# Moving Wout's second-half products of unit 0 three states apart from its gate, and two sums that take in more tiles, in a state-space block with a feed-forward block

## The chip, the cores and the metric

The program runs on one core of one Trainium2 chip. The metric is the device time of one execution in microseconds (us); for the kernel before it is the median of 3 runs, 1132.78 us (1132.46 to 1133.34). A core has five engines that run side by side, each through its own queue in the order of the program: TensorE (PE, matrix products), VectorE (DVE), ScalarE (ACT), GpSimd (POOL) and SyncE (SP, which only issues transfers here). They wait for each other through semaphores.

## The reference

The layer normalises `x` (4 batches of 512 rows of 512), and adds to `x` the output of a Mamba block and of a gated feed-forward block in fp8. Cut to what matters:

```python
def step(h, inp):                      # per time step, per channel (1024), per state (16)
    dA_t, dBu_t, C_t = inp
    h = dA_t * h + dBu_t
    y = jnp.einsum('bdn,bn->bd', h, C_t)
    return (h, y)
...
y = y + hs * D[None, :, None]
y = y * _silu(gate)
out = jnp.einsum('bdl,hd->blh', y, Wout)
...
activations = gelu(x8 @ w_gating[0]) * (x8 @ w_gating[1])   # fp8 operands
ffn = activations @ w_linear                                 # fp8 operands
return x + out + ffn
```

## The kernel before, in words

The program has two parts. `block_a` (to about 235 us) prepares everything; `block_b` runs the scan and all that depends on it, and the change is in `block_b` alone.

The 1024 channels are 8 tiles of 128. A **unit** is one tile `k` (0 to 7) of one batch `b` (0 to 3): 32 units in a row. In each unit there are 16 **states** `n`. For each state ACT makes `da` in a PSUM bank (an exponential, line 896), POOL makes `dbu` (a product, line 938) and DVE runs the scan over 512 time steps (line 995). Eleven states are multiplied by C on DVE (`prod`, line 964). Five, those of `POOLED` = 1, 4, 7, 9, 12, are scanned into `hp` and multiplied on POOL (line 949), `POOL_LAG` = 3 states later. PE sums all 16 products into the bank `yT` by transposing them against an identity (`add_state`, line 1115). When a unit is summed, ACT copies the sum to `y_t` (line 863), PE transposes it back (`back`, line 1033, at state 4 of the next unit), and DVE multiplies it by the gate into `y2` (`gated`, line 970, at state 7 of the next unit). `y2` holds 8 tiles, one for each unit of the batch.

Beside the scan PE makes other products into two PSUM banks `mm`. Which group is made at which state is written in tables, and `pe_pieces` (line 591) turns them into lists: an entry `first` puts a group's four parts at the states `first - 1` to `first + 2` of the unit, and entries at 0 or below come ahead of state 0. The groups:

- `ffn`: the fp8 products of the feed-forward (line 1073), six in unit 0. ACT copies each out of its bank (line 904), the first at its state 10, the sixth at state 15.
- `gate`: four f32 products (line 1085), read by ACT's Silu at state 6 of the next unit.
- `out_a`: Wout times tiles 0 to 3 of `y2`, for the four tiles `h` of the output, in units 5 and 6 of the same batch; DVE adds each to `acc` (line 976, at the states in `OUT_A_ADDED`).
- `out_b`: Wout times tiles 4 to 7, with the feed-forward's output added through an identity (`add_ffn`, line 1044), in units 0 to 3 of the next batch; DVE adds each to `acc` (line 982, at the states in `OUT_B_ADDED`) and SP stores it. It can't begin before unit 7's tile is in `y2`, which comes at state 7 of unit 0.
- `lin`: the feed-forward's second fp8 product (line 1094).

`bank_plan` (line 612) hands the two banks to the groups in turn, in the order of their first parts, and `take_bank` makes PE wait at a group's first part until the bank's last group has been read. All of it is one queue on PE: a part that waits holds up what is behind it, the summing of states too. DVE likewise takes a sum's addition in its place among the scans, and waits there if the sum isn't done. In batch 0 there is no `out_b` in units 0 to 3, since no batch went before.

In the last batch nothing follows unit 7. Its second half is begun inside unit 7 by `LAST` and `begin_last` (line 1124), in four banks named by `last_banks`, and the end of the program makes the rest: `back` for unit 7, tile 7's products, `add_ffn`, four additions and four stores.

Of the kernel before, what the change touches and what calls it, by code (L numbers as in the profile page):

```python
# [21 lines left out]
B, L, H = 4, 512, 512  # L22
# [3 lines left out]
HT = H // P  # L26
LT = L // P
KU = DI // P
# [16 lines left out]
SLOTS = 4  # L45
# [16 lines left out]
HIDS = (3, 3, 3, 3, 4)  # L62
FFN_UNITS, MOST = len(HIDS), max(HIDS)
FFN, FFN_COPIED = (5, 5, 5, 5, 4), (10, 10, 10, 10, 8)
OUT_B, OUT_B_ADDED = (11, -3, -3, -3), {(1, 0): 0, (1, 5): 1, (2, 5): 2, (3, 5): 3}
GATE = (12, 11, 11, 11, 12, 12, 12, 3)
OUT_A_LIN = {4: (), 5: (("out_a", 0, -3), ("out_a", 1, 4), ("lin", 0, 6), ("lin", 1, 9)),
             6: (("out_a", 2, -3), ("out_a", 3, 4), ("lin", 2, 7)), 7: (("lin", 3, 6),)}
MADE = {group[:2]: k for k in OUT_A_LIN for group in OUT_A_LIN[k]}
OUT_A_ADDED = {(5, 5): 0, (5, 9): 1, (6, 5): 2, (6, 9): 3}  # L70
LIN_COPIED = {(5, 14): 0, (6, 1): 1, (6, 15): 2, (7, 14): 3}
GELU_USED, PORT_GIVEN = 4, 4
BACK = 4

LAST = {8: ((1, 4),), 9: ((1, 5), (1, 6)), 11: ((0, 4), (0, 5)), 12: ((0, 6),), 13: ((3, 4), (3, 5)), 14: ((3, 6), (2, 4)),
        15: ((2, 5),)}


def build(nc, x, xT, win_hs, win_gate, wdt, wx, cols, alog, wffn, wout, outT):
# [546 lines left out]
def block_b(nc, xT, win_gate, wout, outT, ident, neg_a, skip, ahead, dram):  # L626
# [9 lines left out]
    plan = bank_plan()  # L636
    with ExitStack() as ctx:
# [34 lines left out]
        da = [ps(f"da{i}", [P, L]) for i in range(SLOTS)]  # L672
        yT = [ps(f"yT{i}", [P, L]) for i in range(2)]
        mm = [ps(f"mm{i}", [P, L]) for i in range(BANKS)]
        last_banks = [mm[plan[(KU - 1, "lin", HT - 1)][0]], yT[0], mm[plan[(KU - 1, "gate", 0)][0]], da[12 % SLOTS]]

        wout_loaded, wlin_loaded = sem("wout_loaded"), sem("wlin_loaded")
        b_loaded = [sem(f"b_loaded{g}") for g in range(G)]
# [9 lines left out]
        y_t_ready, back_mm, y2_ready = sem("y_t_ready"), sem("back_mm"), sem("y2_ready")  # L688
# [339 lines left out]
        def _(pe):  # L1028
# [4 lines left out]
                    ins = nc.tensor.transpose(yT[k % 2][:, t * P:(t + 1) * P], y_t[:, t * P:(t + 1) * P], ident[:, :])  # L1033
                ins.then_inc(back_mm, 1)

            def project_out(bank, h, c, first):
                return nc.tensor.matmul(bank[:, :], wout_sb[:, c, h * P:(h + 1) * P], y2[:, c, :],  # L1037
                                        start=(c == first), stop=(c == KU // 2 - 1))

            def add_ffn(bank, b, h):  # L1040

# [17 lines left out]
            def beside(b, k, piece, opening):  # L1059

                name, h, c = piece
                if name == "out_b" and opening:
                    return
                if name == "ffn":
# [5 lines left out]
                    bank = take_bank(b, k, (name, h), opening)  # L1070
                    pe.sem_inc(waited, 1)
                    for f in range(HT):
                        ins = nc.tensor.matmul(bank[:, :], wffn[:, k % 2, j, f, s, :].bitcast(FP8), xn8[:, f, :].bitcast(FP8),  # L1073
                                               start=(f == 0), stop=(f == HT - 1))
# [4 lines left out]
                bank = group_bank[name]  # L1079
                if name == "gate":  # L1080
                    if c == 0:
                        pe.wait_ge(wgate_loaded[k % 2], unit_loads(b, k))
                        if k == 0:
                            pe.wait_ge(xnT_loaded, b * 16 + 16)
                    ins = nc.tensor.matmul(bank[:, :], wgate[:, k % 2, c * P:(c + 1) * P], xnT[:, c, :],  # L1085
                                           start=(c == 0), stop=(c == 3))
                    done = gate_mm
                elif name == "lin":
                    if c == 0:
                        pe.wait_ge(wlin_loaded, b * 16 + 16)  # L1090
                        pe.wait_ge(act8_ready, b * FFN_UNITS + FFN_UNITS)
                        pe.sem_inc(waited, 1)
                    for i in range(4 * c, 4 * c + 4):
                        ins = nc.tensor.matmul(bank[:, :], wlin[:, i, h * P:(h + 1) * P].bitcast(FP8), act8[:, i, :].bitcast(FP8),  # L1094
                                               start=(i == 0), stop=(i == HID // P - 1))
                    done = lin_mm
                elif name == "out_a":
                    if c == 0:
                        pe.wait_ge(wout_loaded, 16)
                        pe.wait_ge(y2_ready, b * KU + KU // 2)  # L1100
                    ins = project_out(bank, h, c, 0)
                    done = out_a_mm
                else:
                    if c == 0:
                        pe.wait_ge(y2_ready, b * KU)
                    ins = project_out(bank, h, KU // 2 + c, KU // 2)
                    if c == 3:
                        ins = add_ffn(bank, b - 1, h)
                    done = out_b_mm
# [7 lines left out]
                return ins  # L1117

            def begin(h, c):
                project_out(last_banks[h], h, c, KU // 2)  # L1120

            def begin_last(n):

                if n == 8:
                    pe.wait_ge(y2_ready, B * KU - 1)
                if n == 11:
                    pe.wait_ge(lin_copied, B * HT)
                if n == 13:
                    pe.wait_ge(scanned, (B * KU - 1) * N + 12 + 1)
                if n == 14:  # L1130
                    pe.wait_ge(sg_ready, B * KU)
                for h, c in LAST[n]:
                    begin(h, c)
# [36 lines left out]


            back(B * KU - 1, KU - 1)
            begin(2, 6)
            pe.wait_ge(y2_ready, B * KU)
            for h in range(HT):
                project_out(last_banks[h], h, KU - 1, KU // 2)
# [36 lines left out]
```

## Time and profile before

| what | value |
| --- | --- |
| median of 3 runs | 1132.78 us |
| the profiled execution: its time | 1132.28 us |
| the profiled execution: its span | 1130.5 us |
| busy over the span | DVE 92%, POOL 82%, PE 81%, ACT 69% |
| busy in 459 to 682 us, 223 us of the scan | DVE 217.46, POOL 208.74, PE 185.01, ACT 158.24 us |
| TensorE's granted clock, mean | 0.929 of 2.4 GHz |

The span runs from the first to the last instruction; the execution's own time is 1.8 us longer. A timeline row has the start in us, the duration in us, the engine, the line, the instruction, output and input, and a count where equal instructions were merged. Brackets give the idle time of the engine just before it and what ended that. Two instructions of one engine overlap by some 0.1 us where the next begins as the last drains, so a row of two scans of 1.21 us each reads 2.33 us. An f32 product of 128x512 is two MATMUL records (x2), a fp8 one is four for a whole sum (x4), a state's sum is four transposes (x4).

### The profile page before, as it was taken

How to read it: one execution, taken by the hardware profiler on the slowest of the kernel's cores; microseconds unless marked ns; L12 is line 12 of the kernel's file. 1: busy time of each engine (PE TensorE's matmuls, PEld its weight loads, DVE VectorE, ACT ScalarE, POOL GpSimd, SP SyncE). 2: the span in 40 equal slices, each digit the busy share in tenths (PEclk: the TensorE clock that was granted, in tenths of full speed). 3: DMA queues.
4: the chain of work that ended last, by engine and by line, in shares of the span. 5: the costliest groups of instructions: out<-in, count | busy, mean ns of one | idle time of the engine just before them, and what ended most of it. 6: DMA issues, size and time to landing. Idle time of an engine off the chain costs nothing.

```text
span 1130.5 us, 14619 instructions
## 1 busy us (share of the span) xinstructions
PE 921.0 (81%) x4272; PEld 568.1 (50%) x4272; DVE 1041.6 (92%) x1242; ACT 782.7 (69%) x1118; POOL 928.4 (82%) x752
## 2 busy tenths in 40 slices
PE   4878789757777897888888978887988798878988
PEld 3646466334444454555444554444554454454544
DVE  6968777679999999999999999999999999999995
ACT  4687877657778666777785557777856677778552
POOL 5343425489999999989998999999999989999993
PEclk9999999968889999799989989999899899989999
DMA  7677777981111217432212183421212922212101
GB/s 273 207 255 230 285 221 290 374 334 53 52 57 38 84 38 261 177 117 70 75 38 68 55 299 120 130 75 57 71 51 70 347 90 72 75 57 75 38 1 38
DMA packets 53158, 150.24 MB, mean 133 GB/s; under 512 B 5728, under 2 KB 14048, under 8 KB 50016
## 3 DMA queue, kind: packets, MB, share of 16 engines
q1 hardware_dynamic: 53088, 149.41, 38.4%
q8 instruction: 32, 0.52, 0.2%
q14 instruction: 38, 0.31, 0.1%
HBM read 111.37 MB, written 38.01 MB: 132 GB/s over the span
## 4 chain that ended last, share of the span: by engine, by line
POOL 51%; DVE 14%; issue 7%; PE 5%; ACT 1%; DVEq 0%; POOLq 0%
POOL dbu L938 38%; POOL hp L949 14%; DVE hp L995 4%; DVE da L995 3%; DVE prod L964 3%; DVE gate_bf L1011 2%; DVE act L1014 2%; PE mm L1037 2%; PE yT L1115 1%; PE mm L1085 1%; ACT da L896 0%; PE mm L1094 0%; PE da L1037 0%; PE yT L1037 0%; ACT unit L858 0%
## 5 line engine op out<-in xcount | busy, mean ns | idle before, releaser
L896 ACT ACTIVATE da<-unit,neg_a 128x512 f32<-128x512 f32 x512 | 339.0, 683 | 216.5 <-DVE prod L964 215.9
L938 POOL TENSOR_TENSOR dbu<-unit,b_head 128x512 f32<-128x512 f32 x384 | 478.1, 1279 | 3.5 <-POOLq L103 3.5
L995 DVE TENSOR_TENSOR_SCAN da<-da,dbu 128x512 f32<-128x512 f32 x352 | 418.5, 1215 | 8.3 <-POOL dbu L938 6.7
L1115 PE MATMUL yT<-ident,prod 128*128 128x128 f32 x1408 | 237.3, 298 | 138.5 <-DVE prod L964 137.9
L1115 PEld LDWEIGHTS yT<-ident,prod 128*128 128x128 f32 x1408 | 174.9, 151 | 272.8 <-DVE prod L964 220.6
L949 POOL TENSOR_TENSOR hp<-hp,c_head 128x512 f32<-128x512 f32 x128 | 163.4, 1277 | 52.3 <-DVE act L1014 46.3
L995 DVE TENSOR_TENSOR_SCAN hp<-da,dbu 128x512 f32<-128x512 f32 x160 | 193.0, 1206 | 7.9 <-ACT da L896 7.9
L964 DVE TENSOR_TENSOR prod<-da,c_head 128x512 f32<-128x512 f32 x256 | 170.5, 666 | 0.0
L938 POOL TENSOR_TENSOR dbu<-unit,b_all 128x512 f32<-128x512 f32 x128 | 160.3, 1278 | 0.0
L1073 PE MATMUL mm<-xn_b,w_sb 128*128 128x512 fp8e4 x512 | 150.1, 429 | 3.1 <-ACT gate_bf L904 2.0
L1085 PE MATMUL mm<-xnT_b,wgate 128*128 128x512 f32 x256 | 130.1, 606 | 8.1 <-ACT gate_bf L904 8.0
L1037 PE MATMUL mm<-y,wout_sb 128*128 128x512 f32 x240 | 116.8, 605 | 2.4 <-ACT gate_bf L904 2.4
L1115 PE MATMUL yT<-ident,hp 128*128 128x128 f32 x640 | 104.1, 289 | 0.0
L293 POOL TENSOR_TENSOR hs_lo<-hs,hs_hi 128x512 fp32r<-128x512 f32 x32 | 44.0, 1379 | 63.3 <-ACT hs_hi L475 63.3
L1073 PEld LDWEIGHTS mm<-xn_b,w_sb 128*128 128x128 fp8e4 x512 | 54.3, 110 | 61.1 <-issue 31.3
L296 POOL TENSOR_TENSOR dt_du<-dt_du,hs 128x512 f32<-128x512 f32 x32 | 41.2, 1287 | 49.6 <-DVE dt_du L416 49.2
L1115 PEld LDWEIGHTS yT<-ident,hp 128*128 128x128 f32 x640 | 81.9, 151 | 0.0
L358 DVE SCALAR_TENSOR_TENSOR conv<-proj,cols_sb,conv 128x511 f32<-128x511 f32 (+2 forms) x96 | 71.1, 746 | 8.3 <-ACT conv L457 6.1
L519 PE MATMUL proj<-xnT_lo,win_hi 128*128 128x512 f32 x128 | 55.7, 435 | 12.9 <-DVE conv L358 5.8
L964 DVE TENSOR_TENSOR prod<-da,c_all 128x512 f32<-128x512 f32 x96 | 64.2, 670 | 0.0
L1094 PE MATMUL mm<-act,w_sb 128*128 128x512 fp8e4 x256 | 62.7, 383 | 0.0
L1037 PEld LDWEIGHTS mm<-y,wout_sb 128*128 128x128 f32 x240 | 41.5, 194 | 31.5 <-issue 27.6
(114 smaller groups left out, 1234.2 us busy)
## 6 DMA issues: line engine op xcount, KB each, us to landing
unit<-unit_d SPq DMA_DIRECT2D x32, 768.0 KB, 4.2
unit_d<-dt_du SPq DMA_DIRECT2D x32, 512.0 KB, 2.7
wf<-in_wffn SPq DMA_DIRECT2D x12, 1024.0 KB, 6.9
c_head<-bc_d SPq DMA_DIRECT2D x24, 512.0 KB, 4.1
b_head<-bc_d SPq DMA_DIRECT2D x18, 512.0 KB, 5.0
unit_d<-hs SPq DMA_DIRECT2D x32, 256.0 KB, 6.5
w_sb<-w_d SPq DMA_DIRECT2D x64, 128.0 KB, 3.4
wgate<-in_win_gate SPq DMA_DIRECT2D x32, 256.0 KB, 2.7
```

The source lines that it names most:

```text
L358: ins = nc.vector.scalar_tensor_tensor(out=conv[:, k % 2, back:L], in0=proj[k % 3][:, 0:L - back], scalar=cols_sb[:, k, C_TAP + TAPS - 1 - ...
L519: nc.tensor.matmul(bank, hi, low, start=start, stop=False)
L896: nc.scalar.activation(da[n % SLOTS][:, :], unit[:, k % 2, 0, :], ACT.Exp, scale=neg_a[:, k, n:n + 1]).then_inc(da_ready, 1)
L938: nc.gpsimd.tensor_tensor(dbu[:, n % DBUS, :], unit[:, k % 2, 1, :], b_all[n // NS][:, n % NS, :], ALU.mult).then_inc(dbu_ready, 1)
L949: nc.gpsimd.tensor_tensor(hp[:, i % HPS, :], hp[:, i % HPS, :], c_all[m // NS][:, m % NS, :], ALU.mult).then_inc(hp_ready, 1)
L964: nc.vector.tensor_tensor(prod[:, slot, :], da[n % SLOTS][:, :], c_all[n // NS][:, n % NS, :], ALU.mult).then_inc(prod_ready, 1)
L995: nc.vector.tensor_tensor_scan(state, da[n % SLOTS][:, :], dbu[:, n % DBUS, :], 0.0, ALU.mult, ALU.add).then_inc(scanned, 1)
L1037: return nc.tensor.matmul(bank[:, :], wout_sb[:, c, h * P:(h + 1) * P], y2[:, c, :], start=(c == first), stop=(c == KU // 2 - 1))
L1073: ins = nc.tensor.matmul(bank[:, :], wffn[:, k % 2, j, f, s, :].bitcast(FP8), xn8[:, f, :].bitcast(FP8), start=(f == 0), stop=(f == HT - 1))
L1085: ins = nc.tensor.matmul(bank[:, :], wgate[:, k % 2, c * P:(c + 1) * P], xnT[:, c, :], start=(c == 0), stop=(c == 3))
L1094: ins = nc.tensor.matmul(bank[:, :], wlin[:, i, h * P:(h + 1) * P].bitcast(FP8), act8[:, i, :].bitcast(FP8), start=(i == 0), stop=(i == HI ...
L1115: ins = nc.tensor.matmul(yT[k % 2][:, t * P:(t + 1) * P], product[:, t * P:(t + 1) * P], ident[:, :], start=False, stop=last, is_transpose ...
```

## The change

```diff
-OUT_B, OUT_B_ADDED = (11, -3, -3, -3), {(1, 0): 0, (1, 5): 1, (2, 5): 2, (3, 5): 3}
-GATE = (12, 11, 11, 11, 12, 12, 12, 3)
-OUT_A_LIN = {4: (), 5: (("out_a", 0, -3), ("out_a", 1, 4), ("lin", 0, 6), ("lin", 1, 9)),
+OUT_B, OUT_B_ADDED = (9, -3, -3, -3), {(0, 13): 0, (1, 5): 1, (2, 5): 2, (3, 5): 3}
+GATE = (13, 11, 11, 11, 12, 12, 12, 3)
+OUT_A_LIN = {4: (), 5: (("out_a", 0, -3), ("out_a", 1, 3), ("lin", 0, 6), ("lin", 1, 9)),
...
-OUT_A_ADDED = {(5, 5): 0, (5, 9): 1, (6, 5): 2, (6, 9): 3}
+OUT_A_ADDED = {(5, 5): 0, (5, 9): 1, (6, 5): 2, (6, 11): 3}
...
-LAST = {8: ((1, 4),), 9: ((1, 5), (1, 6)), 11: ((0, 4), (0, 5)), 12: ((0, 6),), 13: ((3, 4), (3, 5)), 14: ((3, 6), (2, 4)),
-        15: ((2, 5),)}
+MORE = {("out_a", 2): 5, ("out_a", 3): 6}
+LAST = {8: ((1, 4),), 9: ((1, 5), (1, 6)), 11: ((0, 4), (0, 5)), 12: ((0, 6),), 13: ((2, 5),), 14: ((2, 6),), 15: ((3, 6),)}
...
-        last_banks = [mm[plan[(KU - 1, "lin", HT - 1)][0]], yT[0], mm[plan[(KU - 1, "gate", 0)][0]], da[12 % SLOTS]]
+        last_banks = [mm[plan[(KU - 1, "lin", HT - 1)][0]], yT[0], da[12 % SLOTS], mm[plan[(KU - 1, "gate", 0)][0]]]
...
-                    ins = project_out(bank, h, c, 0)
+                    more = MORE.get((name, h), KU // 2) if b == B - 1 else KU // 2
+                    ins = project_out(bank, h, c, 0, more - 1)
                     done = out_a_mm
+                    if c == 3:
+                        for extra in range(KU // 2, more):
+                            pe.wait_ge(y2_ready, b * KU + extra + 1)
+                            ins = project_out(bank, h, extra, 0, more - 1)
...
-                project_out(last_banks[h], h, c, KU // 2)
+                project_out(last_banks[h], h, c, MORE.get(("out_a", h), KU // 2))
...
-                if n == 14:
+                if n == 15:
                     pe.wait_ge(sg_ready, B * KU)
...
             back(B * KU - 1, KU - 1)
-            begin(2, 6)
             pe.wait_ge(y2_ready, B * KU)
```

- **Unit 0 of batches 1 to 3**: the four products of `out_b` 0 go from states 10 to 13 to states 8 to 11, the gate from states 11 to 14 to states 12 to 15, and DVE's addition from state 0 of unit 1 to state 13 of unit 0.
- **Unit 5 of every batch**: `out_a` 1 begins one state earlier, at state 2.
- **Unit 6**: DVE adds `out_a` 3 at state 11 and not 9, in every batch. In the last batch `out_a` 2 takes in tile 4 too, and `out_a` 3 tiles 4 and 5, with a wait for each tile.
- **Unit 7 of the last batch**: those three products are gone from states 13 to 15 and from behind `back`, and the banks of output tiles 2 and 3 are exchanged.

PE's queue in unit 0 of batch 1 before, from the fifth and sixth `ffn` sum on (`xn_b` in the names is the normalised input in fp8, `y,wout_sb` a product of `out_b`, `xnT_b,wgate` one of the gate, `prod` and `hp` the sums of states):

```order
L1073 MATMUL mm<-xn_b,w_sb 128x512 x8
L1115 MATMUL yT<-ident,prod 128x128 x4
L1037 MATMUL mm<-y,wout_sb 128x512
L1115 MATMUL yT<-ident,prod 128x128 x4
L1115 MATMUL yT<-ident,hp 128x128 x4
L1037 MATMUL mm<-y,wout_sb 128x512
L1085 MATMUL mm<-xnT_b,wgate 128x512
L1037 MATMUL mm<-y,wout_sb 128x512
L1085 MATMUL mm<-xnT_b,wgate 128x512
L1115 MATMUL yT<-ident,prod 128x128 x4
L1115 MATMUL yT<-ident,hp 128x128 x4
L1037 MATMUL mm<-y,wout_sb 128x512
```

and the same stretch now:

```order
L1073 MATMUL mm<-xn_b,w_sb 128x512 x4
L1037 MATMUL mm<-y,wout_sb 128x512
L1073 MATMUL mm<-xn_b,w_sb 128x512 x4
L1037 MATMUL mm<-y,wout_sb 128x512
L1120 MATMUL yT<-ident,prod 128x128 x4
L1037 MATMUL mm<-y,wout_sb 128x512
L1120 MATMUL yT<-ident,prod 128x128 x4
L1120 MATMUL yT<-ident,hp 128x128 x4
L1037 MATMUL mm<-y,wout_sb 128x512
L1044 MATMUL mm<-ffn_bf,ident_bf 128x512
L1085 MATMUL mm<-xnT_b,wgate 128x512
```

The two `ffn` sums stood together, and the `out_b` products were shared out behind them among the gate's. Now the first `out_b` product stands between the two `ffn` sums, the other three follow without any of the gate's among them, and the gate begins behind `out_b`'s end. The row of L1044 ends `out_b` 0 in both (before, it follows the last row shown).

DVE's queue in the same unit before, from state 12 to state 0 of unit 1 (the scans of the trace's line 995 are called SCALAR_TENSOR_TENSOR here):

```order
L995 SCALAR_TENSOR_TENSOR hp<-da,dbu 128x512
L964 TENSOR_TENSOR prod<-da,c_head 128x512
L995 SCALAR_TENSOR_TENSOR da<-da,dbu 128x512 x2
L964 TENSOR_TENSOR prod<-da,c_all 128x512
L995 SCALAR_TENSOR_TENSOR da<-da,dbu 128x512
L964 TENSOR_TENSOR prod<-da,c_all 128x512
L995 SCALAR_TENSOR_TENSOR da<-da,dbu 128x512
L964 TENSOR_TENSOR prod<-da,c_all 128x512
L982 TENSOR_TENSOR acc<-mm,acc 128x512
```

and now:

```order
L995 SCALAR_TENSOR_TENSOR hp<-da,dbu 128x512
L964 TENSOR_TENSOR prod<-da,c_head 128x512
L995 SCALAR_TENSOR_TENSOR da<-da,dbu 128x512
L982 TENSOR_TENSOR acc<-mm,acc 128x512
L995 SCALAR_TENSOR_TENSOR da<-da,dbu 128x512
L964 TENSOR_TENSOR prod<-da,c_all 128x512
L995 SCALAR_TENSOR_TENSOR da<-da,dbu 128x512
L964 TENSOR_TENSOR prod<-da,c_all 128x512
L995 SCALAR_TENSOR_TENSOR da<-da,dbu 128x512
```

The addition to `acc` stood behind state 0's scan of unit 1 and the product of state 15. It now stands between the scans of states 13 and 14.

PE's queue at the end of the last batch before, from state 13 of unit 7 to `back`:

```order
L1115 MATMUL yT<-ident,prod 128x128 x4
L1115 MATMUL yT<-ident,hp 128x128 x4
L1037 MATMUL da<-y,wout_sb 128x512 x2
L1115 MATMUL yT<-ident,prod 128x128 x4
L1037 MATMUL da<-y,wout_sb 128x512
L1037 MATMUL mm<-y,wout_sb 128x512
L1115 MATMUL yT<-ident,prod 128x128 x4
L1115 MATMUL yT<-ident,hp 128x128 x4
L1037 MATMUL mm<-y,wout_sb 128x512
L1033 MATMUL yT<-ident,y_t 128x128 x4
L1037 MATMUL mm<-y,wout_sb 128x512 x2
```

and now:

```order
L1120 MATMUL yT<-ident,prod 128x128 x4
L1120 MATMUL yT<-ident,hp 128x128 x4
L1037 MATMUL da<-y,wout_sb 128x512
L1120 MATMUL yT<-ident,prod 128x128 x4
L1037 MATMUL da<-y,wout_sb 128x512
L1120 MATMUL yT<-ident,prod 128x128 x4
L1120 MATMUL yT<-ident,hp 128x128 x4
L1037 MATMUL mm<-y,wout_sb 128x512
L1033 MATMUL yT<-ident,y_t 128x128 x4
L1037 MATMUL mm<-y,wout_sb 128x512
```

Four products (`y,wout_sb`) stood ahead of the last state's sum, and there are two now. One stands behind it, as before, and behind `back` (L1033) there is one ahead of `add_ffn` where there were two, since the one that was begun there is gone.

## Rows read from the trace of the kernel before

**Rows 1.** page, chain of work that ended last, shares of the span

```profile
POOL 51%; DVE 14%; issue 7%; PE 5%; ACT 1%; DVEq 0%; POOLq 0%
```

**Rows 2.** waits from 235 us on: engine, line <- releaser: us, times, longest

```profile
DVE acc L982 <- PE mm L1044: 5.9, 5, 1.4
...
DVE acc L976 <- PE mm L1037: 2.3, 3, 0.8
```

**Rows 3.** timeline of DVE, units 0/1, batch 1: start, us, engine, line, op [idle]

```profile
473.97 2.33 DVE L995 TENSOR_TENSOR_SCAN da<-da,dbu 128x512 f32<-128x512 f32 x2
...
479.65 0.67 DVE L964 TENSOR_TENSOR prod<-da,c_all 128x512 f32<-128x512 f32 x1
481.67 0.69 DVE L982 TENSOR_TENSOR acc<-mm,acc 128x512 f32<-128x512 f32 x1 [1.35 <-PE mm L1044]
```

**Rows 4.** timeline of PE, the same stretch

```profile
465.56 1.03 PE L1073 MATMUL mm<-xn_b,w_sb 128*128 128x512 fp8e4 x4
466.42 0.60 PE L1115 MATMUL yT<-ident,prod 128*128 128x128 f32 x4
...
474.24 1.13 PE L1037 MATMUL mm<-y,wout_sb 128*128 128x512 f32 x2 [0.80 <-ACT gate_bf L904]
475.20 0.60 PE L1115 MATMUL yT<-ident,prod 128*128 128x128 f32 x4
475.64 0.60 PE L1115 MATMUL yT<-ident,hp 128*128 128x128 f32 x4
...
480.39 1.02 PE L1037 MATMUL mm<-y,wout_sb 128*128 128x512 f32 x2
481.25 0.38 PE L1044 MATMUL mm<-ffn_bf,ident_bf 128*128 128x512 bf16 x1
```

**Rows 5.** timeline of ACT, the same stretch

```profile
473.61 0.58 ACT L904 ACTIVATE gate_bf<-mm 128x512 bf16<-128x512 f32 x1
```

**Rows 6.** timeline of POOL, the same stretch

```profile
483.56 1.27 POOL L949 TENSOR_TENSOR hp<-hp,c_head 128x512 f32<-128x512 f32 x1 [0.95 <-DVE hp L995]
```

**Rows 7.** timeline of DVE, the same add in batch 3

```profile
922.57 0.69 DVE L982 TENSOR_TENSOR acc<-mm,acc 128x512 f32<-128x512 f32 x1 [1.35 <-PE mm L1044]
```

**Rows 8.** line 1011 on DVE: duration ns min/median/max, first and last start

```profile
L1011 DVE TENSOR_TENSOR gate_bf<-gate_bf,up_bf x20: 945/947/2543, 266.8 to 1041.7; 128x1536 bf16<-128x1536 bf16 x16, 128x2048 bf16<-128x2048 bf16 x4
```

**Rows 9.** timeline of DVE, unit 5 of batch 1

```profile
613.15 0.69 DVE L976 TENSOR_TENSOR acc<-mm,acc 128x512 f32<-128x512 f32 x1 [0.83 <-PE mm L1037]
```

**Rows 10.** timeline of PE, unit 5 of batch 1

```profile
608.43 1.91 PE L1037 MATMUL mm<-y,wout_sb 128*128 128x512 f32 x2
...
612.02 1.02 PE L1037 MATMUL mm<-y,wout_sb 128*128 128x512 f32 x2
```

**Rows 11.** windows: busy us (x) by engine, then PEclk (granted clock), DMA share, GB/s

```profile
475.00:480.00 5.00, 5.00 (x22) 2.83 (x21) 5.00 (x7) 4.94 (x6) 5.00 (x5) 1.00 0.00 0
...
607.00:611.00 4.00, 3.76 (x13) 1.99 (x14) 4.00 (x6) 1.99 (x3) 4.00 (x4) 0.61 0.02 4
```

**Rows 12.** timeline of PE, unit 6 of the last batch

```profile
1085.21 0.66 PE L1115 MATMUL yT<-ident,prod 128*128 128x128 f32 x4 [1.05 <-DVE prod L964]
```

**Rows 13.** timeline of all engines, end of the program

```profile
1114.30 1.26 DVE L964 TENSOR_TENSOR prod<-da,c_all 128x512 f32<-128x512 f32 x2
...
1115.44 1.88 PE L1037 MATMUL da<-y,wout_sb 128*128 128x512 f32 x4
...
1117.60 1.02 PE L1037 MATMUL da<-y,wout_sb 128*128 128x512 f32 x2
...
1118.46 1.02 PE L1037 MATMUL mm<-y,wout_sb 128*128 128x512 f32 x2
...
1119.32 0.60 PE L1115 MATMUL yT<-ident,prod 128*128 128x128 f32 x4
...
1120.39 0.60 ACT L863 ACTIVATE y_t<-yT 128x512 f32<-128x512 f32 x1 [7.33 <-PE yT L1115]
...
1122.48 0.30 PEld L1037 LDWEIGHTS mm<-y,wout_sb 128*128 128x128 f32 x2 [0.75 <-DVE y L970]
```

More of the change, by code:

```diff
@@ L1034, in back, with project_out @@
                 ins.then_inc(back_mm, 1)
-            def project_out(bank, h, c, first):
+            def project_out(bank, h, c, first, last=KU // 2 - 1):
                 return nc.tensor.matmul(bank[:, :], wout_sb[:, c, h * P:(h + 1) * P], y2[:, c, :],
-                                        start=(c == first), stop=(c == KU // 2 - 1))
+                                        start=(c == first), stop=(c == last))
             def add_ffn(bank, b, h):
```

## The prediction

> **What bounds the kernel now.** I read the busy time of a stretch first: in 223 us of the scan DVE is busy 217.46 us, POOL 208.74 us. Then the chain of waits, which gives POOL 51% and DVE 14% [rows 1] and so seems to say that POOL sets the pace. The timeline of DVE decides it. Around the change DVE goes from one instruction to the next without a gap, and never waits for POOL there; the gap that it has ends with PE's sum for its addition [rows 3]. POOL is the one that waits, until DVE has scanned state 1 of unit 1 [rows 6]: it is three states ahead and can't go further. So DVE's own queue is the path, and each microsecond that DVE stands still in it is paid in full unless another wait shrinks. What DVE stands still for is read from the waits: the second half's addition, line 982, waits 5.9 us in 5 places [rows 2]. Three of them are the addition at the head of unit 1, each 1.35 us [rows 3, 7]; the other two lie in the end of the program. The first half's addition, line 976, waits 2.3 us in 3 places, 0.83 us at the most [rows 2]; that longest one is in unit 5 of batch 1 [rows 9], and the other two are the same addition in batches 3 and 0.
>
> **Unit 0: what goes.** The product of state 15 starts at 479.65, and an instruction behind a product starts 0.59 us later (0.67 less the overlap), so the addition could start at 480.24. It started at 481.67 [rows 3]. Its wait costs 1.43 us in each of batches 1 to 3. The addition itself, about 0.6 us, is moved and not saved.
>
> **Unit 0: what comes.** DVE's addition now stands behind state 13's scan. The two scans of the row at 473.97 take 2.33 us, one 1.21, so the second starts 1.12 us behind the first [rows 3]. DVE would therefore take the addition at 475.09.
>
> When is the sum done? PE's queue is in order, and the sixth `ffn` sum now goes into the bank of the fifth, so it waits until ACT has copied that one. That copy starts at 473.61 and lasts 0.58 us [rows 5], and it can't move: ACT makes it behind state 14's exponential, which waits for DVE's product of state 10. In the kernel before it is what PE's first `out_b` product waited for, and PE went on at 474.24 [rows 4]. From there PE now has, ahead of the end of `out_b` 0 (the order of its queue stands in the section on the change):
>
> - the sixth `ffn` sum: 0.86 us between the starts at 465.56 and 466.42, and 0.10 us more for the first instruction behind a wait (474.24 to 475.20 for a product that takes 0.86 us elsewhere, as from 480.39 to 481.25) [rows 4]. 0.96 us
> - three `out_b` products, 3 x 0.86 = 2.58 us
> - three sums of states (10, 11 and `hp` 7), each 0.44 us, from 475.20 to 475.64 [rows 4]. 1.32 us; their inputs are there by then, since DVE's scan behind state 11's product starts at 473.97 [rows 3]
>
> That is 4.86 us, so the product with the identity starts at 479.10. Before, it started at 481.25 and the addition at 481.67, 0.42 us later [rows 3, 4]. The addition starts at 479.52, and DVE stands still for 479.52 - 475.09 = 4.43 us, which the profile will show as 4.35. The sum itself comes two states earlier than before by the clock's 2.15 us, but DVE now asks for it 5.15 us earlier.
>
> What is queued behind it on DVE: state 14's scan and all others. POOL, three states ahead, runs into the wait for state 1's scan, and its 0.95 us [rows 6] becomes about 3.9. ACT has the exponentials of states 14 and 15 and of unit 1's state 0 ready. PE's gate waits for the addition, and then finds states 13 to 15 late too, since DVE made them late; by DVE's clock it is where it was. So nobody has anything to give back, and a batch costs 4.43 - 1.43 = 3.00 us. Three batches: **+9.0 us**.
>
> The new wait has no row of its own. Its bounds: below, 1.35 us, what the same addition waits today [rows 3], if PE somehow had its backlog made up; above, 9.3 us, if PE did its 4.86 us of work at half clock. I take the worked-out 4.43, since every piece has a row of the same stretch.
>
> In batch 0 there is no `out_b`, but the sixth `ffn` sum waits for the fifth's copy as well. Its own copy comes up to 0.6 us later, then the Gelu and unit 1's state 1, which DVE would wait for up to 0.4 us. Behind it lies the product of line 1011, which took 2.54 us there and 0.95 usually [rows 8], because POOL was still at work; 1.6 us of cover. I take 0, bounds 0 and 0.4.
>
> The Trainium skill (GPSIMD Engine Reference, section 1, Specifications) says that GpSimd's SBUF interfaces are shared with VectorE and contend with DVE instructions that have two SBUF inputs. By that rule the 2.54 us of line 1011 is a wait for POOL, and the delay of batch 0 vanishes in it; without the rule it costs 0.4 us.
>
> **Unit 5.** `out_a` 1's last product started at 612.02 in batch 1, and the addition at 613.15 [rows 9, 10]. One state earlier, the last product takes the place of the third, at 608.43, and even there at half clock (1.91 us for the pair against 1.02 [rows 10], the granted clock of that stretch being 0.61 [rows 11]) it is done by 610.4, 1.9 us before DVE asks at 612.24. The bank is free in time: PE waits for the Silu that reads it, but in a part of the unit in which it is idle for some microseconds anyway. The waits go: 2.3 us, and 0.08 us of overlap for each of the three: **-2.55 us**. PE does one product less in its busy stretch behind it (0.86 us), so it keeps up with the earlier DVE.
>
> **Unit 6.** In the last batch PE does three products more here, 2.6 us. It waits for DVE 1.05 us at 1085.21 [rows 12] and twice for less shortly before, and has caught up there; the additions come at state 5, with 0.7 us to spare, and at 11, well behind. The addition's move from 9 to 11 is free: no wait stood at 9, and the gate, which wants the bank, begins on PE behind state 11's product. Cost 0, bounds 0 and 0.3.
>
> **The end.** DVE's last two products start at 1114.30 and are done at 1115.6, but PE sums state 15 only at 1119.32 and ACT takes the sum at 1120.39 [rows 13]. PE is the path from 1115.44 on. Between the sums of states 13 and 15 there are four products (1115.44 x4, 1117.60 x2, 1118.46 x2), 0.86 us each, and now two: **-1.72 us**. The product behind `back` that goes saved nothing: PE waited 0.75 us for `y2` behind it [rows 13]. The exchange of banks changes only the order of the last two of four equal steps.
>
> **Sum.** +9.0 - 2.55 - 1.72 = +4.7 us. 1132.28 + 4.7 = 1137.0 us for the profiled execution; the median of before is 0.5 us above its profiled execution, so 1137.5 us. A tenth of a per cent is 1.1 us, and a measurement of this kernel can tell about 0.2%, 2.3 us, from no change.
>
> **The rivals.**
>
> *The stall is covered, as POOL sets the pace.* For it: 51% of the chain is POOL's [rows 1]. Then DVE's 4.43 us lie in slack, and of the change only gains are left: 1132.8 - 4.3 - 2.55 - 1.72 = 1124.2 us. Against it: POOL waits for DVE at just this place [rows 6], and can't be both late and waiting. It decides from a wait of 2.85 us down: there the addition's new wait is repaid by 1.43 us at unit 1 and 4.27 / 3 = 1.42 us of other gains, and the kernel is no slower. With the wait at its lower bound of 1.35 us it is 1128.3 us. Faster in all: 8%.
>
> *PE is partly ahead of my sum*, or the wait is 3 to 3.6 us for a reason that I don't see: 1133 to 1135 us. 10%.
>
> *Half clock.* PE's idle gap ahead of the sixth `ffn` sum grows from 0.80 us [rows 4] to about 1.4, and a new one of 0.7 us stands ahead of the gate. In unit 5 PE came out of a longer gap at 0.61 of its clock, the level of 1.2 GHz for part of it; around 475 to 480 it was 1.00, 2.4 GHz [rows 11]. At the lower level the 4.86 us double: +4.9 us in each batch so hit, 1142.4 us for one and 1152 for all three. For it there is only that longer gap; the same stretch was at full clock in all three batches. 5%.
>
> The Trainium skill (TensorE: Matmul & The Clock Gate, Part 1) has it that the throttled clock is the default and that activity releases it; by that rule, a kernel that adds gaps to PE may pay for them behind the gap, which is this rival and speaks against the change. The trace agrees at 607 us.
>
> *No gain at the end*, if what binds there is not the four products: 1139.2 us. 5%.
>
> *The forecast*: 72%, with a range of its own of 1136.2 to 1139.
>
> **Numbers.** Time 1137.5 us. From 1134 to 1141 us I hold the forecast, the case without the end's gain and a part of the case in between; left out are the faster case (8%), the lower part of the one in between (about 5%) and half clock (5%). Faster by over 0.2% (under 1130.5): 0.08. Within 0.2% (to 1135.0): 0.11. Slower: 0.81.
>
> **What the profile after would show.** Line 982 with a wait of about 4.35 us at state 13 of unit 0 in batches 1 to 3, and none at the head of unit 1; POOL's wait for state 1's scan at 3.9 us; PE going from the fifth to the sixth `ffn` sum with a wait for ACT in between; line 976 without a wait; `y_t` at the end 1.7 us sooner behind DVE's last product. I am wrong if line 982 waits for less than 2.85 us, if DVE begins to wait for POOL elsewhere, or if the scan's durations change.

## The result, and the profile after

The changed kernel takes 1137.52 us (median of 8 runs, 1134.41 to 1139.54), against 1132.65 us for the kernel before (8 runs, 1130.15 to 1133.37). The ratio is 1.0045, with a 95% interval of 1.0033 to 1.0056: it is slower, by about 5 us. The profiled execution took 1137.13 us with a span of 1135.3 us, 4.8 us longer than before. The forecast was 1137.5 us.

The waits of the changed kernel, from 235 us on (engine and line, releaser, us in total, times, longest), are the answer to [rows 2]:

```profile
DVE acc L982 <- PE mm L1044: 14.8, 5, 4.3
POOL hp L949 <- DVE hp L995: 14.1, 8, 4.0
...
PE mm L1085 <- DVE acc L982: 2.4, 3, 0.8
```

The second half's addition waits 14.8 us where it waited 5.9. The first half's waits 0.5 us once where it waited 2.3 us in three places. POOL waits longer for DVE. PE waits for DVE at the gate, which it didn't before.

DVE in unit 0 of batch 1, the stretch of [rows 3]:

```profile
473.07 1.22 DVE L995 TENSOR_TENSOR_SCAN da<-da,dbu 128x512 f32<-128x512 f32 x1
478.60 0.69 DVE L982 TENSOR_TENSOR acc<-mm,acc 128x512 f32<-128x512 f32 x1 [4.31 <-PE mm L1044]
479.21 1.22 DVE L995 TENSOR_TENSOR_SCAN da<-da,dbu 128x512 f32<-128x512 f32 x1
480.34 0.67 DVE L964 TENSOR_TENSOR prod<-da,c_all 128x512 f32<-128x512 f32 x1
```

State 13's scan is done at 474.3. DVE then stands still for 4.31 us, adds, and goes on with state 14. In batches 2 and 3 the same row reads 4.32 and 4.31. There is no wait at the head of unit 1 any more.

PE in the same stretch, the answer to [rows 4] (here the `ffn` and `out_b` rows after the fourth `ffn` sum):

```profile
469.99 1.02 PE L1073 MATMUL mm<-xn_b,w_sb 128*128 128x512 fp8e4 x4 [0.23 <-ACT gate_bf L904]
471.00 1.12 PE L1037 MATMUL mm<-y,wout_sb 128*128 128x512 f32 x2
473.43 1.02 PE L1073 MATMUL mm<-xn_b,w_sb 128*128 128x512 fp8e4 x4 [1.31 <-ACT gate_bf L904]
474.29 1.02 PE L1037 MATMUL mm<-y,wout_sb 128*128 128x512 f32 x2
475.15 0.60 PE L1120 MATMUL yT<-ident,prod 128*128 128x128 f32 x4
475.59 1.02 PE L1037 MATMUL mm<-y,wout_sb 128*128 128x512 f32 x2
476.45 0.60 PE L1120 MATMUL yT<-ident,prod 128*128 128x128 f32 x4
476.89 0.60 PE L1120 MATMUL yT<-ident,hp 128*128 128x128 f32 x4
477.32 1.02 PE L1037 MATMUL mm<-y,wout_sb 128*128 128x512 f32 x2
478.18 0.38 PE L1044 MATMUL mm<-ffn_bf,ident_bf 128*128 128x512 bf16 x1
479.35 1.13 PE L1085 MATMUL mm<-xnT_b,wgate 128*128 128x512 f32 x2 [0.78 <-DVE acc L982]
```

The fifth `ffn` sum, an `out_b` product, 1.31 us of waiting for ACT's copy, the sixth sum, and then the work that the forecast had listed: from 473.43 to the product with the identity at 478.18 it is 4.75 us (forecast 4.86). At 479.35 the gate begins, after PE has stood idle for 0.78 us.

POOL in the same stretch, the answer to [rows 6]:

```profile
485.65 1.27 POOL L949 TENSOR_TENSOR hp<-hp,c_head 128x512 f32<-128x512 f32 x1 [3.95 <-DVE hp L995]
```

POOL's wait for state 1's scan has grown by 3.00 us, which is what DVE lost on balance.

Unit 6 of the last batch, where a wait is new. PE, from its way out of the idle stretch in unit 5 to unit 6:

```profile
1054.95 1.12 PE L1120 MATMUL yT<-ident,prod 128*128 128x128 f32 x4 [3.06 <-DVE prod L964]
1055.85 1.06 PE L1120 MATMUL yT<-ident,hp 128*128 128x128 f32 x4
1056.71 1.92 PE L1037 MATMUL mm<-y,wout_sb 128*128 128x512 f32 x2
1058.41 1.91 PE L1094 MATMUL mm<-act,w_sb 128*128 128x512 fp8e4 x4
...
1074.80 4.46 PE L1037 MATMUL mm<-y,wout_sb 128*128 128x512 f32 x10
1079.10 0.60 PE L1151 MATMUL yT<-ident,unit 128*128 128x128 f32 x4
```

and DVE at the addition of `out_a` 2:

```profile
1077.60 1.22 DVE L995 TENSOR_TENSOR_SCAN da<-da,dbu 128x512 f32<-128x512 f32 x1
1079.37 0.69 DVE L976 TENSOR_TENSOR acc<-mm,acc 128x512 f32<-128x512 f32 x1 [0.55 <-PE mm L1037]
```

PE comes out of 3.06 us of idle time at half speed: four transposes take 1.12 and 1.06 us (0.60 to 0.66 at full clock), two records of a product 1.92 us (1.02). The granted clock there was 0.50 over 3 us and 0.63 over the next 4 (rows below); between the two levels, 1.2 and 2.4 GHz, that is the lower one for about 6 of the 7 us. In the kernel before the same stretch was back at 2.4 GHz sooner:

```profile
1049.19 1.92 PE L1037 MATMUL mm<-y,wout_sb 128*128 128x512 f32 x2
1050.90 1.39 PE L1094 MATMUL mm<-act,w_sb 128*128 128x512 fp8e4 x4
```

The product took 1.92 us there too, but the `lin` product behind it 1.39 and not 1.91 us (1.03 at full clock). In the changed kernel PE has no gap from there up to the five products of `out_a` 2 at 1074.80 (x10), and DVE waits 0.55 us for their end. The granted clock of that stretch (us in the stretch, busy us and counts by engine, then PEclk, DMA share, GB/s):

```profile
1055.00:1058.00 3.00, 3.00 (x10) 2.20 (x11) 3.00 (x4) 1.92 (x3) 3.00 (x4) 0.50 0.00 0
1058.00:1062.00 4.00, 4.00 (x14) 1.97 (x13) 4.00 (x6) 1.30 (x2) 4.00 (x4) 0.63 0.00 0
1062.00:1067.00 5.00, 5.00 (x30) 3.04 (x29) 5.00 (x6) 3.01 (x5) 5.00 (x5) 1.00 0.02 5
...
473.00:479.00 6.00, 5.13 (x23) 2.77 (x23) 1.69 (x3) 5.33 (x7) 6.00 (x6) 1.00 0.00 1
```

The end of the program, the answer to [rows 13]:

```profile
1121.19 1.26 DVE L964 TENSOR_TENSOR prod<-da,c_all 128x512 f32<-128x512 f32 x2
...
1121.95 1.02 PE L1037 MATMUL da<-y,wout_sb 128*128 128x512 f32 x2
...
1123.25 1.02 PE L1037 MATMUL da<-y,wout_sb 128*128 128x512 f32 x2
...
1124.11 0.60 PE L1120 MATMUL yT<-ident,prod 128*128 128x128 f32 x4
...
1125.18 0.60 ACT L863 ACTIVATE y_t<-yT 128x512 f32<-128x512 f32 x1 [5.24 <-PE yT L1120]
```

Two products stand between the sums of states 13 and 15 where there were four. ACT takes the sum 3.99 us after DVE's last two products begin, where it was 6.09 us [rows 13].

The same marks in the two traces give the balance. Each row is by how much the changed kernel is later at a mark than before:

| mark | before, us | after, us | later by | step |
| --- | --- | --- | --- | --- |
| batch 0, unit 1, line 1014 | 269.51 | 269.16 | -0.35 | (ahead already) |
| batch 0, unit 5, second addition | 392.06 | 390.93 | -1.13 | -0.78 |
| batch 1, state 7 of unit 0, `y2` | 466.00 | 465.10 | -0.90 | +0.23 |
| batch 1, unit 1, line 1014 | 489.63 | 491.72 | +2.09 | +2.99 |
| batch 1, unit 5, second addition | 613.15 | 614.34 | +1.19 | -0.90 |
| batch 2, unit 1, line 1014 | 710.72 | 714.89 | +4.17 | +2.98 |
| batch 3, unit 1, line 1014 | 930.54 | 937.69 | +7.15 | +2.98 |
| batch 3, unit 5, second addition | 1053.69 | 1059.94 | +6.25 | -0.90 |
| batch 3, unit 6, first addition | 1072.49 | 1079.37 | +6.88 | +0.63 |
| end, ACT takes the sum | 1120.39 | 1125.18 | +4.79 | -2.09 |

Unit 0: +8.95 us. Unit 5: -2.58 us. Unit 6: +0.63 us. The end: -2.09 us. What is left, -0.12 us, is the 0.35 us of head start and 0.23 us that are lost in unit 6 of batch 0: there ACT waits 0.53 us for PE's sum, behind a slow stretch of PE like the one above, and a scan of DVE begins 0.81 us behind the addition before it where it was 0.59.

### The profile page after: what moved, and what is told of

The parts are those of the page before. It is cut to its first block, busy times and chain, and to the rows that moved or that the text cites. A ratio compares the mean times of both kernels' runs of the same rounds, so it can differ in the third digit from the quotient of the medians.

```text
span 1135.3 us, 14622 instructions
## 1 busy us (share of the span) xinstructions
PE 920.9 (81%) x4272; PEld 565.7 (50%) x4272; DVE 1043.0 (92%) x1242; ACT 782.8 (69%) x1118; POOL 928.1 (82%) x752
## 4 chain that ended last, share of the span: by engine, by line
POOL 48%; DVE 16%; issue 9%; PE 5%; ACT 2%; DVEq 0%; POOLq 0%
POOL dbu L938 35%; POOL hp L949 13%; DVE da L995 5%; DVE hp L995 3%; DVE prod L964 3%; DVE gate_bf L1011 2%; DVE act L1014 2%; PE mm L1037 1%; PE yT L1120 1%; ACT da L896 1%; PE mm L1094 1%; ACT gate_bf L874 0%; PE mm L1085 0%; PE yT L1037 0%; DVE y L970 0%
## 5 line engine op out<-in xcount | busy, mean ns | idle before, releaser
L1073 PE MATMUL mm<-xn_b,w_sb 128*128 128x512 fp8e4 x512 | 146.6, 420 | 13.5 <-ACT gate_bf L904 12.1
L519 PE MATMUL proj<-xnT_lo,win_hi 128*128 128x512 f32 x128 | 55.7, 435 | 10.6 <-ACT xnT L438 4.3
```

The lines of the kernel that those rows point to most:

```text
L519: nc.tensor.matmul(bank, hi, low, start=start, stop=False)
```

## The experiments

All ran in 5 rounds beside the kernel before; ratios are to it, with their 95% intervals. Theory A is the forecast's: DVE's queue is the path, and it pays for each wait of an addition. Its rival B puts the loss in PE's new order or has it covered by POOL; rival C blames the gate, which shares a bank with `out_b` 0.

**1. The edits of unit 0 alone.** On the kernel before:

```diff
-OUT_B, OUT_B_ADDED = (11, -3, -3, -3), {(1, 0): 0, ...
-GATE = (12, ...
+OUT_B, OUT_B_ADDED = (9, -3, -3, -3), {(0, 13): 0, ...
+GATE = (13, ...
```

> The kernel before with only the edits of unit 0 (out_b 0 at states 8 to 11, the gate at 12 to 15, the addition at state 13). Theory A (DVE's queue is the path, and the addition at state 13 waits for a sum that PE can't finish earlier): 3 x 3.0 us more than before, about 1141.5 us, ratio 1.008; line 982 waits 4.3 us in units 0 of batches 1 to 3, line 976 keeps its waits of 0.65 to 0.83 us in unit 5. Rival B (the unit-0 edits are covered by POOL, and the 4.9 us come from elsewhere, such as the longer sums of unit 6): no more than 1133 us. Rival C (the gate's later place costs as much as the addition): more than 1143 us, with waits of ACT for the gate.

Measured: 1142.38 us against 1132.17, ratio 1.0093 (1.0073 to 1.0113). The interval holds A's 9.0 us (1.0079) and excludes B. The waits of line 982 are 4.32, 4.31 and 4.32 us. C can't be told from A by this time alone, but its sign, ACT waiting for the gate, is not in the trace. The waits of line 976 in unit 5 stayed, but not as foreseen: 0.63, 0.83, 2.05 and 0.52 us in batches 0 to 3. Here is batch 2, where the kernel before had none:

```profile
841.10 0.69 DVE L976 TENSOR_TENSOR acc<-mm,acc 128x512 f32<-128x512 f32 x1 [2.05 <-PE mm L1037]
```

PE's clock (the same columns as above) was at half from 835 to 838 us in that trace:

```profile
835.00:838.00 3.00, 3.00 (x9) 1.50 (x8) 3.00 (x5) 1.30 (x2) 3.00 (x3) 0.50 0.00 0
```

**2. All the other edits alone.** The changed kernel with the two lines of unit 0 as they were:

```diff
-OUT_B, OUT_B_ADDED = (9, -3, -3, -3), {(0, 13): 0, ...
-GATE = (13, ...
+OUT_B, OUT_B_ADDED = (11, -3, -3, -3), {(1, 0): 0, ...
+GATE = (12, ...
```

> The changed kernel with unit 0 put back as it was before; what stays is out_a 1 a state earlier, out_a 3 added at state 11, and the three products moved out of the last unit. Theory A: the two gains without the loss: 2.6 us in unit 5 and about 2 us at the end, less 0.6 us for a new wait of out_a 2's addition in unit 6 of the last batch: 1132.65 - 4.0 = about 1128.7 us, ratio 0.9965. Rival B (the gains of unit 5 and of the end are taken back by something else, and unit 0 costs only 4.9 us in all): 1132.7 us.

Measured: 1127.65 us against 1132.17, ratio 0.9960 (0.9945 to 0.9974), 4.5 us faster where A had 4.0. B is out: the gains are real and not taken back. The two halves of the change, +10.2 and -4.5 us, make +5.7 us, and the whole made +4.9; the intervals of the halves are wider than that difference. The trace has the waits of 1.35 us at the head of unit 1 again, and the 0.53 us of `out_a` 2's addition in unit 6.

**3. The addition at state 15.** In the changed kernel:

```diff
-OUT_B, OUT_B_ADDED = (9, -3, -3, -3), {(0, 13): 0, ...
+OUT_B, OUT_B_ADDED = (9, -3, -3, -3), {(0, 15): 0, ...
```

> The changed kernel with the addition of out_b 0 at state 15 of unit 0 in place of 13. PE's queue is as in the changed kernel. Theory A: DVE does two scans and two products (3.4 us) before it asks for the sum, so the wait falls from 4.3 to 0.9 us in each of three batches and the time by 10.2 us, to 1127.3 us. Rival B (the loss lies in PE's new order, the sixth ffn sum and the gate, and not in where DVE waits): 1137 us, with the wait moved to the products or scans behind. Rival C (the gate, which waits on PE for the addition, becomes late): over 1130 us, with ACT waiting for the gate in unit 1.

Measured: 1126.37 us, ratio 0.9951 (0.9932 to 0.9970). PE's queue is word for word that of the changed kernel, and yet the 5 us of loss have become 6 us of gain. DVE in unit 0 of batch 1:

```profile
476.84 0.67 DVE L964 TENSOR_TENSOR prod<-da,c_all 128x512 f32<-128x512 f32 x1
478.41 0.69 DVE L982 TENSOR_TENSOR acc<-mm,acc 128x512 f32<-128x512 f32 x1 [0.90 <-remote]
```

("remote" where the view names no engine as the releaser.) The sum is ready at the same time, 478.4 against 478.6; DVE has done two scans and two products more before it asks, and waits 0.90 us where it waited 4.31. Ratios differ by 0.0094, 10.6 us, for 10.2 us of wait. This is what separates A from B: the loss is where DVE stands, not what PE does. C, which had over 1130 us and ACT waiting for the gate, is out as well; there is no such wait in the trace.

**4. The addition at state 0 of unit 1**, where the kernel before had it:

```diff
-OUT_B, OUT_B_ADDED = (9, -3, -3, -3), {(0, 13): 0, ...
+OUT_B, OUT_B_ADDED = (9, -3, -3, -3), {(1, 0): 0, ...
```

> The changed kernel with the addition of out_b 0 back at state 0 of unit 1, its place in the kernel before; PE's queue as in the changed kernel. Theory A: the sum is done 0.7 us before DVE asks, so no wait at all: 13.2 us less than the changed kernel, about 1124.3 us, ratio 0.9926 to before. Rival C (the gate shares a bank with out_b 0, so PE stands at the gate's first product until the addition and holds up the sums of states 13 to 15): y_t of unit 0 comes later in unit 1, ACT waits there 1 to 3 us, and the time is 1126 us or more. Rival B (the loss lies in PE's order): 1137 us.

Measured: 1125.35 us, ratio 0.9936 (0.9915 to 0.9957), 1 us above the expectation. The interval reaches 1127.3 us, so the time alone doesn't exclude C's 1126 or more. No wait of line 982 is left at the head of unit 1. Both of C's signs are there: PE stands at the gate and ACT waits for the sum of unit 0. The two rows of these waits, and DVE's wait for ACT (the same columns as above):

```profile
DVE hp L995 <- ACT da L896: 10.7, 20, 1.3
ACT y_t L863 <- PE yT L1120: 10.3, 4, 5.9
...
PE mm L1085 <- DVE acc L982: 5.2, 3, 1.7
```

ACT's 10.3 us hold 5.9 at the end of the program, so about 1.5 us in each of three batches. These three don't reach DVE: behind them it next waits for ACT in unit 2, 0.39 us, as in every kernel. DVE waits for ACT 10.7 us in all, 20 times, where the fifth kernel waits 7.9 us, 16 times. The four more are state 1 of unit 1 in each batch, ahead of ACT's wait for the sum: 0.50 us in batches 1 to 3, because the sixth `ffn` sum is copied late, and 1.31 us in batch 0, which costs nothing there (see batch 0 below). So the gate's place costs nothing that can be seen, and the copy of the sixth sum 0.5 us a batch.

**5. `out_b` 0 from state 9 on, with the addition at state 0 of unit 1.** Against the fourth:

```diff
-OUT_B, OUT_B_ADDED = (9, -3, -3, -3), {(1, 0): 0, ...
+OUT_B, OUT_B_ADDED = (10, -3, -3, -3), {(1, 0): 0, ...
```

> As the run with the addition at state 0 of unit 1 (1125.35 us), but out_b 0 begins at state 9 in place of 8, behind both ffn sums; the gate stays at 12. Then the sixth ffn sum doesn't wait for the copy of the fifth, and the gate doesn't wait for the addition. Theory A (only DVE's waits count): out_b 0 is done at the same time, since a product takes the place of the sixth ffn sum in PE's 4.86 us, so line 982 still doesn't wait; the wait of state 1's scan for ACT in unit 1 falls from 0.50 to about 0.4; 1125 us, no more than 1 us less. Rival (PE's wait for the addition, 1.7 us at the gate, and ACT's 1.5 us for the sum cost something further on): 1 to 4 us less, 1121 to 1124 us.

Measured: 1124.76 us against 1132.39, ratio 0.9933 (0.9913 to 0.9953), so no more than 1 us below the fourth, as A has it. PE no longer waits for an addition, ACT waits 0.31 us for that sum and not 1.49, and the wait of 0.50 us at state 1 of unit 1 is gone. A part of this gain is taken back by another thing. Line 1011 on DVE in this kernel (duration ns min/median/max, first and last start):

```profile
L1011 DVE TENSOR_TENSOR gate_bf<-gate_bf,up_bf x20: 946/1226/2566, 265.3 to 1035.2; 128x1536 bf16<-128x1536 bf16 x16, 128x2048 bf16<-128x2048 bf16 x4
```

and in the changed kernel:

```profile
L1011 DVE TENSOR_TENSOR gate_bf<-gate_bf,up_bf x20: 945/947/1995, 267.0 to 1048.8; 128x1536 bf16<-128x1536 bf16 x16, 128x2048 bf16<-128x2048 bf16 x4
```

In unit 1 of batch 1 of the fifth kernel, DVE's row:

```profile
484.86 1.22 DVE L1011 TENSOR_TENSOR gate_bf<-gate_bf,up_bf 128x1536 bf16<-128x1536 bf16 x1
```

and POOL's:

```profile
481.54 3.73 POOL L938 TENSOR_TENSOR dbu<-unit,b_head 128x512 f32<-128x512 f32 x3
```

DVE has come so close behind POOL that it starts line 1011 at 484.86 while POOL is at work until 485.27. The product takes 1.22 us and not 0.95, and 1.27 and 1.24 us in the same unit of batches 2 and 3. These three alone move the median of the 20 from 947 to 1226 ns: of batch 0, the four with 1536 columns are stretched in every kernel here, and the four products with 2048 columns take 1.22 to 1.27 us in every one. Against the fourth kernel's trace, DVE gains 0.6 us in each of batches 1 to 3 ahead of line 1011 (the 0.50 us wait for ACT) and loses 0.3 us of it there, 0.9 us on balance.

**6. `out_a` 2 added at state 6 of unit 6**, on top of the fifth:

```diff
-OUT_A_ADDED = {(5, 5): 0, (5, 9): 1, (6, 5): 2, (6, 11): 3}
+OUT_A_ADDED = {(5, 5): 0, (5, 9): 1, (6, 6): 2, (6, 11): 3}
```

> As the run before it, with out_a 2 added at state 6 of unit 6 in place of 5. Theory A (DVE waits 0.55 us there in the last batch since PE comes late, with five products in the sum and after a stretch at half clock in unit 5): that wait goes and nothing else changes, 0.6 us less, which such a measurement can't tell from nothing; the trace shows no wait of line 976. Rival (lin 2, which takes the bank, then begins late and holds PE up): no gain or a loss of up to 1 us, with PE waiting for DVE ahead of lin 2.

Measured: 1124.92 us, ratio 0.9939 (0.9920 to 0.9959). No difference from the fifth can be told, as expected. Its trace shows no wait of line 976, but that of the fifth shows none either; the wait comes and goes with PE's clock in unit 5, so this run doesn't show that the edit is worth anything. The rival's sign, PE waiting for DVE ahead of `lin` 2, is not there either.

**7. Unit 5 alone.** On the kernel before:

```diff
-OUT_A_LIN = {4: (), 5: (("out_a", 0, -3), ("out_a", 1, 4), ("lin", 0, 6), ("lin", 1, 9)),
+OUT_A_LIN = {4: (), 5: (("out_a", 0, -3), ("out_a", 1, 3), ("lin", 0, 6), ("lin", 1, 9)),
```

> The kernel before with only out_a 1 one state earlier in unit 5. Theory A: the waits of line 976 go (2.3 us, and 0.08 us of overlap for each): 2.6 us less than before, 1129.6 us, ratio 0.9977. Rival (POOL or PE takes the place of the wait within the unit): no difference, with POOL's or PE's waits for DVE smaller by as much.

Measured: 1128.83 us against 1132.39, ratio 0.9973 (0.9957 to 0.9988). 3.1 us by the ratio, 2.6 expected, and the interval excludes the rival's no difference. No wait of line 976 is left.

**8. As 6, on the fourth kernel** (`out_b` 0 from state 8):

```diff
-OUT_A_ADDED = {(5, 5): 0, (5, 9): 1, (6, 5): 2, (6, 11): 3}
+OUT_A_ADDED = {(5, 5): 0, (5, 9): 1, (6, 6): 2, (6, 11): 3}
```

> As the run with the addition of out_b 0 at state 0 of unit 1, with out_a 2 added at state 6 of unit 6 in place of 5; out_b 0 still begins at state 8. Theory A: 0.6 us less than that run, about 1124.7 us, and as much above the variant whose out_b begins at state 9 as the three waits of state 1's scan for ACT make, 0.3 to 1.2 us. Rival (the place of out_b's start counts for more): 2 us or more between the two.

Measured: 1126.13 us, ratio 0.9950 (0.9932 to 0.9968), against the fourth's 0.9936. The 0.6 us were not seen; the intervals overlap. Inconclusive.

**9. The edits for the last batch alone.** The second kernel with `out_a` 1 of unit 5 put back:

```diff
-             5: (("out_a", 0, -3), ("out_a", 1, 3), ("lin", 0, 6), ("lin", 1, 9)),
+             5: (("out_a", 0, -3), ("out_a", 1, 4), ("lin", 0, 6), ("lin", 1, 9)),
```

> The kernel before with only the edits for the last batch: the sums of out_a 2 and 3 take in three more tiles, out_a 3 is added at state 11 of unit 6, and the last unit makes two products less ahead of its last sum. Theory A: y_t at the end comes 1.7 to 2.1 us sooner behind DVE's last product. In unit 6 PE is now 0.86 us later than where out_a 1 has gone a state earlier, and DVE 0.9 us later too, so out_a 2's addition waits about as in the changed kernel, 0 to 0.6 us: 1.2 to 2 us less than before, about 1130.9 us, ratio 0.9985 to 0.999. Rival (the three products cost as much in unit 6 as they save at the end): no difference, with a wait of 1.5 us or more at out_a 2's or out_a 3's addition.

Measured: 1131.65 us against 1132.97, ratio 0.9987 (0.9973 to 1.0000), within the expected 1.2 to 2 us but with an interval that reaches no change. The mechanism is in the trace: DVE's last two products start at 1116.52 and ACT takes the sum at 1120.94, 4.42 us later and not 6.09; 1.67 us sooner, just under the 1.7 expected. Neither addition of unit 6 waits, so the rival's sign is missing, though the time doesn't exclude it. In this trace the additions in unit 5 wait 0.83, 0.83, 2.00 and 1.96 us, 5.6 us where the kernel before had 2.3 in its one profiled execution.

## Why the prediction was right, point by point

- **DVE's queue is the path.** Right, and shown by the third run: the same work on every engine, the addition two states later on DVE, 10.6 us less. The chain of waits had POOL at 51% [rows 1] and has it at 48% now, for the same work on POOL: it can run through either of two engines that go in step, and only the gaps in their timelines tell which one sets the pace.
- **The new wait.** Forecast 4.43 us, to be shown as 4.35; shown as 4.31, 4.32 and 4.31. PE's piece was 4.75 us and not 4.86: the 0.10 us for the first instruction behind a wait, taken from an `out_b` product, wasn't paid by the `ffn` sum. Unit 0 cost 8.95 us against 9.0.
- **Batch 0.** The sixth `ffn` sum came late as foreseen and state 1's scan waited 0.47 us (0.4 forecast as the bound). The changed kernel was 0.35 us ahead before that and 0.35 us ahead behind line 1011: the delay vanished there, where the longest duration is 1995 ns and was 2543 [rows 8]. In both traces that product ends 0.82 us behind the end of POOL's instruction, so here POOL sets the pace, not DVE's queue. The row of the Trainium skill on GpSimd's shared SBUF interfaces (GPSIMD Engine Reference, section 1, Specifications) gave the same, and the fifth run agrees with it with 1.22 us for 0.95 when POOL is at work.
- **Unit 5.** Forecast -2.55, in the trace -2.58. The wait that was taken away is not a constant, though: see the last section.
- **Unit 6.** The miss. It was given 0 to 0.3 us with "0.7 us to spare", and cost 0.63 us. The spare time was read at one clock history. The wait that was taken as PE having caught up (1.05 us at 1085.21 [rows 12]) lies 13 us behind the addition of `out_a` 2, which is at 1072.49 in that trace. It took two things together, a fifth product in the sum and a long slow stretch of PE in unit 5, and the traces have each without the other. Batch 0 of the changed kernel has the same slow stretch with four products, and no wait:

```profile
405.79 3.60 PE L1037 MATMUL mm<-y,wout_sb 128*128 128x512 f32 x8
...
409.72 0.67 DVE L976 TENSOR_TENSOR acc<-mm,acc 128x512 f32<-128x512 f32 x1
```

The granted clock over 8 us behind the gap in unit 5, in batches 0 and 3 of the changed kernel and in batch 3 of the fourth experiment's kernel (the same columns as above):

```profile
385.93:393.93 8.00, 8.00 (x29) 4.81 (x30) 8.00 (x10) 3.27 (x5) 8.00 (x8) 0.63 0.01 2
1054.95:1062.95 8.00, 8.00 (x29) 4.82 (x30) 8.00 (x10) 3.27 (x5) 8.00 (x8) 0.63 0.00 0
...
1043.21:1051.21 8.00, 8.00 (x37) 4.56 (x38) 8.00 (x10) 3.27 (x5) 8.00 (x8) 0.79 0.00 0
```

The kernels of experiments 3, 4 and 5 have five products in batch 3 and a clock of 0.80, 0.79 and 0.81 there: PE begins the sum 5.2 to 5.4 us before DVE asks for it, and there is no wait. In the changed kernel and in the second experiment (0.63 too) PE begins 3.9 to 4.0 us before, and DVE waits 0.55 and 0.53 us. In the ninth the stretch is as slow (0.64) without a wait, but DVE had waited 1.96 us for PE in unit 5. So the term that was too small is unit 6's: it had no part for the clock.

- **The end.** Forecast -1.72, in the trace -2.09: the two products, and 0.38 us because PE was that much less behind DVE in unit 7. The product behind `back` saved nothing, as foreseen: PE now stands idle for 0.79 us there in its stead.
- **Half clock in unit 0**, the rival with 5%: it didn't come in batches 1 to 3. The granted clock from 473 to 479 us is 1.00, with a gap of 1.31 us just before, and it is 1.00 behind the same gaps in batches 2 and 3. A gap that the forecast left out is that of batch 0, where no `out_b` product fills it: 3.29 us ahead of the sixth `ffn` sum. Behind it PE ran at full clock in the changed kernel (1.00 from 255 to 262 us), and mostly at the lower level in the first, third and fourth experiments (0.67, 0.69 and 0.71), where state 1's scan then waited 1.31 to 1.33 us and not 0.47. Line 1011, behind POOL, covered that too: it still ended 0.81 us behind POOL's instruction. The rule behind this rival (the Trainium skill, TensorE: Matmul & The Clock Gate, Part 1) did show itself, in unit 5: the granted clock is 0.50 behind 3.06 us of idle time. It did so unevenly: behind 3.19 us of idle time in unit 5 of batch 2 the kernel before had 1.00.
- **The sum.** 0.35 us of head start and the end's larger gain (0.37 us) were balanced by unit 6 (0.63) and unit 6 of batch 0 (0.23); +4.8 us in the span, for +4.7 forecast. That the small misses cancel, and that the median meets 1137.5 to 0.02 us where the runs lie 5 us apart, is luck. The large term, unit 0, is not: its wait was met within 0.04 us, for the reason given.

## What to carry to other kernels

When an addition is placed in the queue of the engine that is the path, place it by when its input can be ready at the earliest, and count from the last thing that the producer is tied to (here ACT's copy) through all that stands ahead in the producer's queue. At state 13 the addition waited 4.3 us a time here, two states later 0.9 us, and at the head of the next unit not at all. Moving a sum to be ready sooner is of use only if nobody asks for it sooner by more: `out_b` 0 came 2 us earlier and was asked for 5 us earlier. Of this change the parts beside unit 0 are worth keeping (1127.65 us, ratio 0.9960). So is `out_b` 0 begun earlier, once the addition is back at the head of unit 1: with both the kernel takes about 1125 us (1124.76, ratio 0.9933), 0.7% less than before.

## What the runs showed of the hardware that was not expected

- The stretch at half clock behind PE's 3 us of idle time in unit 5 differs from one batch and one execution to the next. The same addition there waited 0.65, 0.83, 0 and 0.83 us in the kernel before, 0.63, 0.83, 2.05 and 0.52 in the first experiment, 0.83, 0.83, 2.00 and 1.96 in the ninth. Their sum is 2.3 us in one execution and 5.6 us in another, so a wait of this kind, read from one execution, can be off by a factor of two. It may be a part of why the runs of one kernel spread (1134.41 to 1139.54 us for the changed one); that wasn't tried.
- VectorE's product of line 1011 (two bf16 inputs in SBUF) is stretched when GpSimd is at work: 0.95 us alone, 1.22 us in the fifth experiment with 0.41 us of overlap, up to 2.57 us with 1.75 us of overlap. In each of these it ends 0.81 to 0.83 us behind the end of GpSimd's instruction. As DVE's waits go, this comes in the place of a part of them: 0.3 us of 0.6 in three batches of the fifth experiment.
